# Output experts of a three-stage transformer pipeline: one mask over both token chunks instead of one for each, read from an SBUF copy of the choice numbers

## The reference

```python
x = _layernorm(x + _L0_attn_ref(x, ...))      # stage A: Mamba-like block, 16 sequences of 256 tokens, 128 wide
x = _layernorm(x + _L0_ffn_ref(x, ...))       # stage B: attention with experts in its values and its output
x = _layernorm(x + _L1_attn_ref(x, ...))      # stage C: linear attention
x = _layernorm(x + _L1_ffn_ref(x, ...))       # stage D: soft mixture of experts over all sequences

# the end of stage B, which the change touches (8 heads of 64, 8 experts)
gates = sigmoid((x @ w_gate)...)
sel = argmax(gates, axis=-1)
gm = one_hot(sel, EXPERTS) * gates
...
out = einsum('bhne,ehkd,bhnk->bhnd', gm, output_experts, out)
return out.sum(axis=1)
```

## Time and profile before

| | us |
|---|---|
| median of 3 runs | 1579.16 (1578.62 to 1583.59) |
| profiled execution, its own time | 1580.04 |
| span of the profiled execution, first to last instruction | 1578.1 |
| PE busy / PE weight loads busy | 1438.5 / 1261.2 |
| DVE busy | 1214.6 |
| ACT busy | 820.8 |
| POOL busy | 790.4 |
| masks, DVE L1360 | 166.3 |
| products of the output experts, PE L636 | 275.8 |

### The profile page before, as it was taken

The page is one execution under the profiler, slowest core; times in us unless marked ns, Lnnn a source line. Parts: engine busy times, 40 slices in busy tenths (PEclk is TensorE's granted clock), DMA queues, the critical chain, the costliest instruction groups (busy, mean ns, idle before and its releaser), DMA issues. The chain is left out here.

```text
span 1578.1 us, 32322 instructions
## 1 busy us (share of the span) xinstructions
PE 1438.5 (91%) x10752; PEld 1261.2 (80%) x10752; DVE 1214.6 (77%) x2335; ACT 820.8 (52%) x1846; POOL 790.4 (50%) x1959
## 2 busy tenths in 40 slices
PE   5588999999999999999999999946999999869997
PEld 4366788788788788788788787836999999869997
DVE  4466798898898898898898887764888888736664
ACT  2234544544544544544544544303777776557774
POOL 0332253553553553553553552222777777557763
PEclk9998999999999999999999999966999999989999
DMA  6000000000000000000000000008676667877782
GB/s 236 7 7 1 8 1 14 15 1 14 15 1 15 15 1 14 15 1 15 15 1 15 8 1 8 8 7 252 171 197 188 185 186 199 254 266 301 300 316 71
DMA packets 140752, 132.10 MB, mean 84 GB/s; under 512 B 7376, under 2 KB 130512, under 8 KB 134096
## 3 DMA queue, kind: packets, MB, share of 16 engines
q1 hardware_dynamic: 140624, 130.50, 26.1%
HBM read 73.85 MB, written 56.62 MB: 83 GB/s over the span
## 5 line engine op out<-in xcount | busy, mean ns | idle before, releaser
L636 PE MATMUL bk<-ve_f,oe 128*128 128x128 f32 x2048 | 275.8, 279 | 0.8 <-DVE ve_f L1360 0.8
L636 PEld LDWEIGHTS bk<-ve_f,oe 128*128 128x128 f32 x2048 | 248.9, 192 | 23.4 <-issue 20.1
L2287 POOL TENSOR_TENSOR d_s<-d_ex 128x1024 f32<-128x1024 f32 x32 | 131.8, 4120 | 100.8 <-ACT d_ex L2087 100.8
L1360 DVE SCALAR_TENSOR_TENSOR ve_f<-ps_m,oT 128x512 f32<-128x512 f32 x248 | 166.3, 678 | 3.7 <-PE bk L636 2.3
L1321 DVE COPY_PREDICATED vals<-oh,bk 128x1024 f32<-128x1024 int32 x112 | 146.6, 1309 | 10.3 <-PE bk L404 8.5
L2037 PE MATMUL d_sl<-d_ex,e_prT 128*128 128x128 f32 x1024 | 136.0, 277 | 8.8 <-POOL d_ex L2304 8.8
L1971 PE MATMUL d_lg<-d_phf,d_xtf 128*128 (+1 forms) x1024 | 128.1, 287 | 14.4 <-DVE d_ex L2191 7.6
L1971 PEld LDWEIGHTS d_lg<-d_phf,d_xtf 128*128 128x128 f32 x1024 | 125.1, 203 | 15.2 <-issue 11.1
L2037 PEld LDWEIGHTS d_sl<-d_ex,e_prT 128*128 128x128 f32 x1024 | 125.4, 193 | 9.0 <-POOL d_ex L2304 9.0
L1981 PE MATMUL d_sl<-d_ex,d_xs 128*128 128x128 f32 x1024 | 121.3, 277 | 5.8 <-DVE d_ex L2202 5.8
L1981 PEld LDWEIGHTS d_sl<-d_ex,d_xs 128*128 128x128 f32 x1024 | 118.4, 194 | 6.2 <-DVE d_ex L2202 6.2
(11 more groups left out here) (340 smaller groups left out, 3730.5 us busy)
## 6 DMA issues: line engine op xcount, KB each, us to landing
logits<-d_raw SPq DMA_DIRECT2D x128, 256.0 KB, 3.3
e_lt<-logits SPq DMA_DIRECT2D x32, 1024.0 KB, 5.1
y_slots<-d_ys SPq DMA_DIRECT2D x64, 256.0 KB, 4.3
d_ex<-y_slots SPq DMA_DIRECT2D x16, 1024.0 KB, 6.8
d_w<-W SPq DMA_DIRECT2D x16, 256.0 KB, 3.4
oe<-xT SPq DMA_DIRECT2D x1, 2048.0 KB, 7.9
xt_in<-xT SPq DMA_DIRECT2D x16, 128.0 KB, 2.3
x_in<-x SPq DMA_DIRECT2D x16, 128.0 KB, 2.4
```

Source lines behind the costliest of these rows:

```text
L636: last = pe.matmul(ps_u[:, cols], oe[:, hp, e, :], mo[:, n % MO, hp, :], start=False, stop=(e == NE - 1 and hp == HP - 1), skip_group_chec ...
L1360: V.scalar_tensor_tensor(mo[:, n % MO, :, :].rearrange("p a n -> p (a n)"), chosen_of(b, c), float(NE - e), oT[:, u, c, :, :].rearrange("p ...
L2287: G.tensor_tensor(s8[:], part[:, 0:8, :], part[:, 8:16, :], ALU.add).then_inc(n, 1)
```

## The change

- `b_mo` makes one mask for both chunks: 128x1024 elements, 8 for a sequence instead of 16 of 128x512. The ring has three such buffers instead of four of half the size.
- The numbers are no longer read by DVE from PSUM. ACT copies them to an SBUF tile `chosen` in bf16 (`b_m`, two copies of 128x512 for a sequence); DVE reads `chosen` and `oT`, both in SBUF.
- `b_out(b, e, half)` works with 256 columns, so that 32 products of 256 columns stand in place of 64 of 128. The four head pairs of an expert are issued as two halves, at the places where the groups of four products of 128 columns stood.
- `b_choice` of chunk 1 moves from the middle of the slot to its start, since both chunks must be there before the first mask.
- Room: `pr` gets memory of its own, several set-up tiles share memory with later ones, `sz` and `yg` are written in place of `tz` and `ya`.

```diff
@@
-MO = 4
-OUTS = C * NE
+MO = 3
...
-        pr = ve_f[:, 2048:3584].rearrange("p (q s a n) -> p q s a n", q=2, s=2, a=3)
+        pr = sb("pr", [2, 2, 3, P])
...
-        oT = sb("oT", [2, C, HP, P])
-
-        mo = ve_f[:, 0:MO * HP * P].rearrange("p (s a n) -> p s a n", s=MO, a=HP)
+        oT = sb("oT", [2, HP, C, P])
+        chosen = sb("chosen", [HP, C, P], BF16)
+
+        mo = ve_f[:, 0:MO * HP * L].rearrange("p (s a n) -> p s a n", s=MO, a=HP)
@@ PE: b_choice
-                if (b, c) != (Z, 1):
-                    wait(pe, q["b_mo"], OUTS * b + NE * c)
-                else:
-                    wait(pe, q["b_pt"], HB * NB)
+                wait(pe, q["b_m"], C * b + c)
...
-                    last = pe.matmul(chosen_of(b, c)[:, hp * P:(hp + 1) * P], pick[rows, hp, :, :].rearrange("p a k -> p (a k)"),
+                    last = pe.matmul(ps_m[:, hp * P:(hp + 1) * P], pick[rows, hp, :, :].rearrange("p a k -> p (a k)"),
@@ PE: b_out
-            def b_out(b, c, e):
-
-                n = NE * c + e
-                cols = slice(c * P, (c + 1) * P)
-                pe.wait_ge(q["b_mo"], OUTS * b + n + 1)
-                for hp in range(HP):
-                    last = pe.matmul(ps_u[:, cols], oe[:, hp, e, :], mo[:, n % MO, hp, :], start=False,
+            def b_out(b, e, half):
+
+                n = NE * b + e
+                if half == 0:
+                    pe.wait_ge(q["b_mo"], n + 1)
+                for hp in (2 * half, 2 * half + 1):
+                    last = pe.matmul(ps_u, oe[:, hp, e, :], mo[:, n % MO, hp, :], start=False,
                                      stop=(e == NE - 1 and hp == HP - 1), skip_group_check=True)
-                last.then_inc(q["b_oe"], 1)
+                if half == 1:
+                    last.then_inc(q["b_oe"], 1)
@@ PE: slot
                 if c:
                     b_oat(t - 3)
+                if o:
+                    b_choice(t - 2, u, 1)
                 if b:
                     b_qk(t - 1, 1 - u, 1)
...
                 if b:
                     b_turn(t - 1, 2)
-                if o:
-                    b_choice(t - 2, u, 1)
                 if b:
                     b_turn(t - 1, 3)
...
@@ ACT
+            def b_m(b, c):
+                act.wait_ge(q["b_m_ps"], C * b + c + 1)
+                wait(act, q["b_mo"], NE * b)
+                copy(chosen[:, :, c, :], ps_m[:].rearrange("p (a n) -> p a n", a=HP)).then_inc(q["b_m"], 1)
...
                 if a:
                     a_lx(t, 0)
+                if o:
+                    b_m(t - 2, 0)
                 if b:
                     b_eg(t - 1)
                     b_qk(t - 1, 0)
                 if a:
                     a_lx(t, 1)
+                if o:
+                    b_m(t - 2, 1)
                 if b:
                     b_qk(t - 1, 1)
@@ DVE: b_mo
-            def b_mo(b, u, c, e):
-
-                n = NE * c + e
+            def b_mo(b, u, e):
+
+                n = NE * b + e
                 if e == 0:
-                    dve.wait_ge(q["b_m_ps"], C * b + c + 1)
-                if n == 0:
+                    dve.wait_ge(q["b_m"], C * (b + 1))
                     dve.wait_ge(q["b_ot"], HP * (b + 1))
-                wait(dve, q["b_oe"], OUTS * b + n - MO + 1)
-                V.scalar_tensor_tensor(mo[:, n % MO, :, :].rearrange("p a n -> p (a n)"), chosen_of(b, c), float(NE - e),
-                                       oT[:, u, c, :, :].rearrange("p a n -> p (a n)"), ALU.is_equal, ALU.mult
+                wait(dve, q["b_oe"], n - MO + 1)
+                V.scalar_tensor_tensor(mo[:, n % MO, :, :].rearrange("p a n -> p (a n)"),
+                                       chosen[:].rearrange("p a c n -> p (a c n)"), float(NE - e),
+                                       oT[:, u, :, :, :].rearrange("p a c n -> p (a c n)"), ALU.is_equal, ALU.mult
                                        ).then_inc(q["b_mo"], 1)
```

More of the change, by code:

```diff
@@ L190, in token_blocks @@
         mx = sb("mx", [C, NH, P])
+        lx_flat = lx[:, :, :, :].rearrange("p c h t -> p (c h t)")
+        mx_flat = mx[:, :, :, :].rearrange("p c h t -> p (c h t)")
+        sv, sa, su, sd, s2, sp = (lx_flat[:, TT * NH * i:TT * NH * (i + 1)].rearrange("p (n h) -> p n h", h=NH)
+                                  for i in range(6))
+        negb_f = mx_flat[:, 0:3 * P].rearrange("p (k n) -> p k n", k=3)
+        out_w0 = mx_flat[:, 3 * P:3 * P + 2 * D].rearrange("p (j d) -> p j d", j=2)
         ep = sb("ep", [NH])
@@ L195, in token_blocks @@
         tz = sb("tz", [C, DI])
-        sz = sb("sz", [C, DI])
+        sz = tz
         ya = sb("ya", [C, DI])
-        yg = sb("yg", [C, DI])
+        yg = ya
         sq = sb("sq", [DI])
@@ L286, in token_blocks @@
             b_g_ps b_eg b_gate b_oht_ps b_oht b_qk_ps b_qk b_v_ps b_v0 b_v b_vg b_s_ps b_max b_p b_pt_ps b_pt
-            b_pv b_rg b_rgs b_rgb_ps b_rgb b_ot b_m_ps b_mo b_oe b_oa b_oat_ps b_x2t_ps b_x2t b_start
+            b_pv b_rg b_rgs b_rgb_ps b_rgb b_ot b_m_ps b_m b_mo b_oe b_oa b_oat_ps b_x2t_ps b_x2t b_start
             c_qk_ps c_g c_km c_q c_v_ps c_v c_rot_ps c_qr c_t2 c_krt_ps c_kr c_kv_ps c_kv c_out_ps c_z c_res c_n
@@ L889, in _ @@
             b_out(Z, 0, 1)
[L890 to L895, removed]
             b_out(Z, 1, 0)
             b_out(Z, 1, 1)
+            b_out(Z, 2, 0)
+            b_out(Z, 2, 1)
+            b_out(Z, 3, 0)
+            b_out(Z, 3, 1)
+            b_out(Z, 4, 0)
+            b_out(Z, 4, 1)
             b_x2t(Y, 0)
-            b_out(Z, 1, 2)
+            b_out(Z, 5, 0)
             c_qk(Y, 0)
-            b_out(Z, 1, 3)
-            b_out(Z, 1, 4)
+            b_out(Z, 5, 1)
+            b_out(Z, 6, 0)
             c_v(Y, 0)
-            b_out(Z, 1, 5)
+            b_out(Z, 6, 1)
             c_rot(Y)
-            b_out(Z, 1, 6)
-            b_out(Z, 1, 7)
+            b_out(Z, 7, 0)
+            b_out(Z, 7, 1)
             c_krt(Y)
@@ L943, in a_tz @@
                 act.wait_ge(q["a_z_ps"], b + 1)
-                wait(act, q["a_sz"], b)
+                wait(act, q["a_yg"], b)
                 nc.scalar.activation(tz[:].rearrange("p c n -> p (c n)"), ps_a[:], ACT.Tanh, scale=0.5
@@ L1173, in _ @@
             slot(NB // 2, 0, False, True, True, True, False)
+            b_m(Z, 0)
+            b_m(Z, 1)
             b_x2t(Y, 0)
@@ L1205, in a_sz @@
                 dve.wait_ge(q["a_tz"], b + 1)
-                wait(dve, q["a_yg"], b)
                 V.scalar_tensor_tensor(sz[:].rearrange("p c n -> p (c n)"), tz[:].rearrange("p c n -> p (c n)"), 1.0,
@@ L1248, in a_y @@
                 dve.wait_ge(q["a_y_ps"], b + 1)
+                wait(dve, q["a_sq"], C * b)
+                wait(dve, q["a_yt_ps"], b)
                 dve.wait_ge(q["a_int"], 2 * b + 2)
@@ L1252, in a_y @@
                 dve.wait_ge(q["a_y"], b + 1)
-                wait(dve, q["a_sq"], C * b)
-                wait(dve, q["a_yt_ps"], b)
                 V.tensor_tensor(yg[:], ya[:], sz[:], ALU.mult).then_inc(q["a_yg"], 1)
@@ L1634, in _ @@
             slot(NB // 2, 0, False, True, True, True, False)
-            b_mo(Z, 1, 0, 0)
-            b_mo(Z, 1, 0, 1)
-            b_mo(Z, 1, 0, 2)
-            b_mo(Z, 1, 0, 3)
-            b_mo(Z, 1, 0, 4)
-            b_mo(Z, 1, 0, 5)
-            b_res(Y)
-            b_mo(Z, 1, 0, 6)
-            b_mo(Z, 1, 0, 7)
-            b_mo(Z, 1, 1, 0)
-            b_mo(Z, 1, 1, 1)
-            b_mo(Z, 1, 1, 2)
-            b_mo(Z, 1, 1, 3)
+            b_mo(Z, 1, 0)
+            b_mo(Z, 1, 1)
+            b_mo(Z, 1, 2)
+            b_res(Y)
+            b_mo(Z, 1, 3)
+            b_mo(Z, 1, 4)
+            b_mo(Z, 1, 5)
             b_x2(Y, 0)
-            b_mo(Z, 1, 1, 4)
-            b_mo(Z, 1, 1, 5)
-            b_mo(Z, 1, 1, 6)
-            b_mo(Z, 1, 1, 7)
+            b_mo(Z, 1, 6)
+            b_mo(Z, 1, 7)
             c_q(Y)
```

75 lines of the change are left out of this document (25 added, 50 removed).

## The result

| | before | after |
|---|---|---|
| median, us | 1579.66 (1578.62 to 1583.59, 4 runs) | 1658.82 (1656.56 to 1660.95, 4 runs) |
| ratio, 95% interval | | 1.0496 [1.0471, 1.0521] |
| span of the profiled execution | 1578.1 | 1659.0 |
| a full slot (slots 3 to 14) | 59.09 on average | 63.07 once, then 64.74 on average |

A forecast was written before the change was run, and what follows sets the result against it. PE was taken to wait at `b_rgb` for a DVE chain with POOL 0.16 us from setting it; 0.4 + 3.6 - 0.16 - 0.05 - 0.1 makes 3.7 us a slot, 48 over 13, plus 1: 1628 us, range 1590 to 1652.

The forecast's parts named there:

- What bounds the kernel: Full slots: PE waits at `b_rgb` for a chain through DVE's `b_max` of pair 3, with DVE and POOL neck and neck.
- The slack of 0.16 us: At `a_ln2`: DVE arrives 0.16 us after POOL's ln2 ends, all the slack POOL has before it sets PE's progress.
- What the masks do to POOL: Masks 2 to 5, over chains rms to ln2: each costs POOL 0.9 us, together 3.6 us at `a_ln2`; chance 0.74.
- The mask's length: On DVE: one mask of 1024 takes 1.15 us against 1.20 for a pair of 512; bounds 0.69 and 1.27.
- Start of the chains later: Start of the slot: four short products moved there make attention values, `a_y` and the rms chain 0.4 us later.
- DVE between the chains: Between `a_ln2` and `b_max`: one long mask in the place of two short ones saves 0.05 us.
- The sum: Full slot: `b_rgb` 3.8 us later, less 0.1 for groups behind it, 3.7 us a slot, 48 us over 13.
- TensorE's clock: Rival: after a wait of about 3 us PE falls to 1.2 GHz, 3 us more a slot, 1667 us; chance 0.05.
- the likeliest case: Loss on POOL as reckoned: 1628 us, reaching from 1608 to 1650; PE's waits grow by 4.6 us a slot; chance 0.74.
- PE's own saving: PE's products: 16 groups save 0.03 us each, five dearer groups 0.4 to 0.5 in all, about 0.9 us a slot.
- Copies on ACT: Two copies of about 0.65 us each fit ACT's waits and cost nothing; without that cover up to 1.3 us a slot.
- Outside the full slots: Partly filled slots cost nothing; in the tail a longer first mask, less 0.5 us saved by PE's groups, gives +1 us.

The follow-up runs named there:

- the run with two steps: Changed kernel with two Newton steps instead of three in every reciprocal root of stages A to C: 1590.93 us, ratio 1.0067.
- the run with the filled wait: Changed kernel with five needless products of 256 columns into `ps_m` ahead of `b_rgb` of pair 2: 1641.67 us, ratio 1.0382.
- the split masks: Changed kernel with each mask made by two instructions of 512 elements, both reading the SBUF copy `chosen`: 1635.82 us, ratio 1.0355.

## Why the prediction was wrong, point by point

- **What bounds the kernel**: right in the main. A delay of POOL's chain reached the slot's end, with the long masks and with five Newton steps; a shorter chain gave nothing in the kernel before, where DVE is the chain; and the short mask moved there made the slot 0.5 us shorter. Two readings were off. The slack of 0.16 us was some 0.05. And `b_rgb` isn't PE's only wait in every slot: one of 0.7 us for ACT's `kr` (L690, 10 times between 300 and 900 us) stands earlier in it.
- **What the masks do to POOL**: right, 3.6 us predicted. The four instructions under masks 2 to 5 take 1.05 to 1.19 us for 0.20, less 0.85 to 0.99 each, 3.7 in all; the stretch from rms to ln2 is 3.4 us longer (24.8 for 21.4). The Trainium skill (SBUF — State Buffer, Who interferes with whom) states the rule; the pair of 0.52 and 0.20 us agrees with it. Its full length for each mask (4.9 us a slot) is too much here, because an instruction's own 0.20 us isn't lost and it starts some way into the mask.
- **The mask's length**: right, 1.15 us predicted, 1.14 from start to start (491.90 to 493.04). One 16-bit input of two gave nothing, as the Trainium skill (VectorE: DVE Perf Modes, What auto-detection actually checks) has it.
- **Start of the chains later, 0.4 us**: mis-sized, 0.82. The 0.4 of the moved choice is there: DVE's `x` of lnB starts 12.04 us into the slot for 11.63. The other 0.4 is added around mask 1. I let masks hold up POOL but not POOL hold up a mask, and mask 1 took 1.76 us beside POOL's addition, 1.68 from start to start where two short masks take 1.2. Moving it gave 1.16 us. The choice was not put back in any run, so its part is read from the trace alone.
- **DVE between the chains**: -0.05 reckoned. I looked at the pair behind `a_ln2` alone; ahead of it three long masks replace five short ones, +0.4. Under the POOL wait this is hidden; in the run with two steps it is seen.
- **The sum**: 3.7 us a slot predicted, 4.0 in the slot without a clock fall (63.07 for 59.09): 0.4 more by the start, 0.1 by the slack, 0.2 less by the masks. Over thirteen slots that is 52 for 48.
- **TensorE's clock**: this is the step that failed. I gave it 0.05, because the clock held with waits up to 1.2 us, and priced it at 3 us a slot for a wait of about 3. My own sum made the waits grow by 4.6 us a slot, most of it at `b_rgb`, so this was a consequence of the likeliest case and no rival to it. PE's idle time in a full slot with the full clock grew by 3.5 us (62.98 - 57.93 for 59.03 - 57.48), 1.7 of it at `b_rgb`, whose wait became 2.48 for 0.82. With that the clock fell in 12 of 13 full slots at 1.66 each, 20 us; the run with the filled wait shows that this was the cause. Without these 20 us it is 1639, inside the range, as the 1642 of that run is. The price was wrong the other way: PE is at the lower level for some 3 us in all, which costs about half of that.
- **PE's own saving, 0.9 us a slot**: wrong, but off the path. A group of four takes 496.65 to 497.52, 0.87 us, 0.02 less than a group of eight; a dear group still takes 1.07 (498.69 to 499.76), so the second weight load was not what made it dear. 16 x 0.02 is 0.3 us. Both rows stand at the end of this section.
- **Copies on ACT, nothing**: right. No wait of PE or DVE for them is in the list; all 128 masks together had 3.0 us of idle time ahead of them, 1.8 of it ended by products (L1362 above).
- **Outside the full slots, +1**: 9 us measured. I took the partly filled slots for free and the tail nearly so; 7 us were in them, and no run takes these apart. The 2 in stage D go with its lower clock.

The trace of the kernel before had a warning for the clock, outside the three slots that I read. In slot 1, which holds only a part of the work, its mean is 0.92, though no wait of PE there is longer than 1.7 us and those near the falls are of 0.6 to 1.2 us:

```profile
84.04:138.69 54.65, 46.14 (x244) 32.99 (x244) 36.34 (x75) 25.65 (x74) 15.82 (x52) 0.92 0.02 6
```

The sum of the differences: 48 predicted in slots, 4 for the mis-sized terms, 20 for the clock and 9 outside give 81, for 80.9 measured. The pitches of PE (start to start) for its own saving:

```profile
496.65 1.03 PE L628 MATMUL bk<-ve_f,oe 128*128 128x256 f32 x4
497.52 0.39 PE L553 MATMUL bk<-negb,id_b 128*128 128x256 bf16 x2
...
498.69 1.13 PE L628 MATMUL bk<-ve_f,oe 128*128 128x256 f32 x4
499.76 0.65 PE L583 MATMUL ps_o<-pt,vals 128*64 128x256 f32 x4
```

What stays open is in which slots the clock falls: the same wait of about 2.5 us was followed by a fall in 12 of 13 full slots of the changed kernel, in every second one with the split masks, and in 5 of 13 with mask 1 moved. Nor does the fall keep its place: by the trace's record of the clock it begins 57.3 us into slot 4 of the changed kernel and 58.5 us into slot 14, a little later each time, while `b_rgb` starts at 57.3 or 57.4 in all of them. So the wait is needed here, but it alone doesn't set the moment.

## What to carry to other kernels

Where VectorE and GpSimd each have work on the critical path, keep one input of VectorE's large operations in PSUM, or put them where GpSimd's small chains don't run; a copy that frees PSUM or halves a width can cost more through the other engine than it saves. When a forecast puts a longer wait on TensorE, add the clock to the sum and not to the rivals, and look at the granted clock slot by slot, not in the mean of the page. And before merging products to help an engine that is 97% busy, read what its longest wait is for: one short mask moved behind one maximum gained 8 us, the whole change lost 79.

## What the runs showed of the hardware that was not expected

- The holding up goes both ways: a VectorE mask of 1.22 us takes 1.76 when GpSimd's addition of 128x256 (0.92 us) starts first.
- Two instructions of half the length cost GpSimd's chain less (0.64 us) than one whole (0.85 to 0.99); it gets one small instruction done with each.
- TensorE's clock fell to the lower level behind a wait of 2.48 us, cost 1.65 us each time, and did so in some slots and not in others that look alike; needless products in the wait prevented it. In slot 1 of the kernel before its mean was 0.92 with no wait above 1.7 us, so a single long wait isn't needed.
